# The program's first tile: loaded by two queues, normalised on three engines, with wk and the mix interleaved by block and wv split on GpSimd

## The reference

```
xn = layernorm(x)
xs = xn shifted by one token;  xm = xn*time_mix + xs*(1 - time_mix)
k = exp(min(xm @ Wk.T, 60));   v = xm @ Wv.T;   r = xm @ Wr.T
rwkv = sigmoid(r) * decayed_sum(k*v) / decayed_sum(k)
w_q = clip(round(W / mean|W|), -1, 1)
out = x + rwkv @ Wo.T + scaled(quantised(layernorm2(xn)) @ w_q)
```

## Time and profile before

| what | value |
|---|---|
| median of 3 runs (lowest to highest) | 893.41 us (892.99 to 894.22) |
| time of the profiled execution | 891.49 us |
| span of its instructions | 889.7 us |
| TensorE matmuls busy | 867.1 us, 97% |
| VectorE busy | 764.8 us, 86% |
| ScalarE, GpSimd busy | 510.3 us (57%), 215.2 us (24%) |
| DMA, mean over the span | 120 GB/s |

### The profile page before, as it was taken

The page is one execution under the profiler, slowest core; times in us unless marked ns, Lnnn a source line. Parts: engine busy times, 40 slices in busy tenths (PEclk is TensorE's granted clock), DMA queues, the critical chain, the costliest instruction groups (busy, mean ns, idle before and its releaser), DMA issues.

```text
span 889.7 us, 12792 instructions
## 1 busy us (share of the span) xinstructions
PE 867.1 (97%) x3984; PEld 714.5 (80%) x3984; DVE 764.8 (86%) x1278; ACT 510.3 (57%) x834; POOL 215.2 (24%) x242
## 2 busy tenths in 40 slices
PE   3989999999999999999999999999999999999998
PEld 2778888888888888888888888888888888888886
DVE  5998999989897999989897897878978888789684
ACT  5584767667594757566564554545546536365441
POOL 5552326242452425240030100200201103011000
PEclk9999999999999999999999999999999999999999
DMA  8222415041423224045643245324451443424311
GB/s 283 108 83 88 149 54 184 13 171 54 165 71 135 101 82 154 12 172 136 212 145 115 84 154 189 125 75 141 153 175 57 157 141 96 154 93 142 95 48 47
DMA packets 59841, 107.13 MB, mean 120 GB/s; under 512 B 7712, under 2 KB 7712, under 8 KB 59808
## 3 DMA queue, kind: packets, MB, share of 16 engines
q1 hardware_dynamic: 59808, 106.73, 35.1%
HBM read 64.76 MB, written 41.96 MB: 120 GB/s over the span
## 4 chain that ended last, share of the span: by engine, by line
PE 90%; DVE 3%; issue 2%; POOL 2%; ACT 1%; DMA 0%; SPq 0%; POOLq 0%; DVEq 0%; ACTq 0%
PE kvr L513 18%; PE kvr L515 18%; PE kvr L514 18%; PE out_banks L552 7%; PE out_banks L554 7%; PE out_banks L534 6%; PE out_banks L533 6%; PE out_banks L531 6%; PE transposed L466 2%; PE out_banks L466 2%; DVE bn_stats L842 1%; POOL normed L1174 1%; POOL own_stats L1156 1%; POOL own_stats L1157 1%; DMA x<-in_x 0%
## 5 line engine op out<-in xcount | busy, mean ns | idle before, releaser
L1247 POOL TENSOR_TENSOR evacuated<-normed,mix_over_ffn_row 128x512 f32<-128x512 f32 x28 | 49.0, 1751 | 339.0 <-DVE ffn_lo L922 339.0
L513 PE MATMUL kvr<-xm_hi,wk_hi 128*128 128x512 f32 x256 | 103.7, 405 | 2.6 <-DVE xm_lo L922 2.6
L513 PE MATMUL kvr<-xm_hi,wv_hi 128*128 128x512 f32 x256 | 102.9, 402 | 2.2 <-DVE wv_lo L927 1.3
L513 PE MATMUL kvr<-xm_hi,wr_hi 128*128 128x512 f32 x256 | 102.7, 401 | 0.0
L515 PE MATMUL kvr<-xm_hi,wk_lo 128*128 128x512 f32 x256 | 101.0, 395 | 0.0
L514 PE MATMUL kvr<-xm_lo,wk_hi 128*128 128x512 f32 x256 | 100.7, 394 | 0.0
L515 PE MATMUL kvr<-xm_hi,wv_lo 128*128 128x512 f32 x256 | 100.2, 391 | 0.0
L515 PE MATMUL kvr<-xm_hi,wr_lo 128*128 128x512 f32 x256 | 100.1, 391 | 0.0
L531 PE MATMUL out_banks<-wo_hi,rwkv_hi 128*128 128x512 f32 x256 | 100.0, 390 | 0.0
L534 PE MATMUL out_banks<-wo_hi,rwkv_lo 128*128 128x512 f32 x256 | 99.7, 389 | 0.0
L514 PE MATMUL kvr<-xm_lo,wr_hi 128*128 128x512 f32 x256 | 99.7, 389 | 0.0
(11 more groups left out here) (140 smaller groups left out, 1922.7 us busy)
## 6 DMA issues: line engine op xcount, KB each, us to landing
other<-ffn_input SPq DMA_DIRECT2D x64, 256.0 KB, 5.1
x<-in_x SPq DMA_DIRECT2D x15, 1024.0 KB, 5.8
other<-in_x SPq DMA_DIRECT2D x8, 1024.0 KB, 5.8
ffn_input<-evacuated SPq DMA_DIRECT2D x32, 256.0 KB, 4.4
ffn_input<-parked SPq DMA_DIRECT2D x32, 256.0 KB, 2.2
attn_scratch<-x SPq DMA_DIRECT2D x8, 1024.0 KB, 4.2
parked<-attn_scratch SPq DMA_DIRECT2D x8, 1024.0 KB, 6.7
out<-parked SPq DMA_DIRECT2D x8, 1024.0 KB, 5.2
```

The source lines that it names most:

```text
L513: nc.tensor.matmul(KVR[:, m, :], hi, XH[t][:, ch, :], start=(ch == 0), stop=False)
L1247: G.tensor_tensor(U[:, n % RING, :], XN[:, ch, :], BC[:, :], ALU.mult).then_inc(pool_v, 1)
```

## The change

The change touches the startup only, apart from waits that TensorE carries in every batch.

- **Loads.** SyncE issues blocks 0 and 2 of the first tile and then the constants; ScalarE issues blocks 1 and 3.
- **First normalisation.** VectorE takes blocks 0 and 1, GpSimd block 2, ScalarE block 3. The second normalisation (for the feed-forward input) of blocks 0 and 1 goes from GpSimd to VectorE.
- **Mix.** The shifted part is written into an own buffer `FIRST` of 513 columns whose first column is zero, so that one instruction per block takes the place of three. The P slots are transposed into the `out_banks`.
- **wk and mix.** ScalarE and VectorE split block m of wk between the steps of the mix; TensorE waits for wk's low part block by block.
- **wv.** The low part of wv moves from VectorE to GpSimd, behind its high part; a semaphore `pool_w` counts it. GpSimd splits wo only when `dve_w` shows wk and wr done. The reload of the second x tile waits for `pool_w`.

```diff
@@ nc.sync
+            for q in (0, 2):
+                sp.dma_start(X[0][:, q, :], x_t[0, 0][:, q, :]).then_inc(s_xq[q], 16)
             sp.dma_start(cst[:, :], constants).then_inc(s_small, 16)
-            for q in range(Q):
-                sp.dma_start(X[0][:, q, :], x_t[0, 0][:, q, :]).then_inc(s_xq[q], 16)
             for n in "kvr":
                 load_weight(n)
             sp.dma_start(ZA[:, :, :], x_t[HALF, 0]).then_inc(s_oth, 16)
             sp.wait_ge(dve_w, CH)
             load_weight("o")
-            sp.wait_ge(dve_w, 2 * CH)
+            sp.wait_ge(pool_w, CH)
             sp.dma_start(X[1][:, :, :], x_t[0, 1]).then_inc(s_x[1], 16)
@@ nc.tensor
-            for normed in (pool_xn, act_xn):
+            for normed in (dve_xn, pool_xn, act_xn):
                 pe.wait_ge(normed, CREDIT)
             for m in range(CH):
                 transpose_slot(0, "P", m, XN)
-            pe.wait_ge(dve_w, CH)
-            pe.wait_ge(dve_x, 2)
...
-                if m:
-                    pe.wait_ge(dve_w, (m + 1) * CH)
+                if m == 1:
+                    pe.wait_ge(pool_w, CH)
+                if m == 2:
+                    pe.wait_ge(dve_w, 2 * CH)
...
                         pe.wait_ge(dve_lo, RING + slots_before(b, ph, slot0 + ch) + 1)
+                        pe.wait_ge(dve_w, ch + 1)
@@ nc.scalar
+            for q in (1, 3):
+                nc.scalar.dma_start(X[0][:, q, :], x_t[0, 0][:, q, :]).then_inc(s_xq[q], 16)
...
-            weight_hi("k")
-            for m in range(CH):
+            weight_hi("k", [0])
+            evacuate(0, "P", 0)
+            weight_hi("k", [1])
+            evacuate(0, "P", 1)
+            high_part(0, "P", 0)
+            for m in range(2, CH):
+                weight_hi("k", [m])
                 evacuate(0, "P", m)
-            for m in range(CH):
-                high_part(0, "P", m)
+                high_part(0, "P", m - 1)
+            high_part(0, "P", CH - 1)
@@ nc.vector
-                    V.tensor_copy(last_x[:, ch:ch + 1], shifted(ph, n)[:, TILE - 1:TILE])
-                    V.tensor_scalar(U[:, r, 0:1], bank[:, 0:1], scale, None, ALU.mult)
-                    V.scalar_tensor_tensor(U[:, r, 1:TILE], bank[:, 1:TILE], scale, shifted(ph, n)[:, 0:TILE - 1],
+                    V.scalar_tensor_tensor(U[:, r, :], bank, scale, FIRST[:, n, 0:TILE],
                                            ALU.mult, ALU.add).then_inc(dve_x, 1)
...
-            weight_lo("k")
+            for q in range(2):
+                last = V.tensor_scalar(XN[:, q, :], X[0][:, q, :], own[:, 0, 0, q:q + 1], own[:, 0, 1, q:q + 1],
+                                       ALU.mult, ALU.add)
+            last.then_inc(dve_xn, 1)
+            weight_lo("k", [0])
             mix_or_clip(0, "P", 0)
             for m in range(1, CH):
+                weight_lo("k", [m])
                 mix_or_clip(0, "P", m)
                 low_part(0, "P", m - 1)
             low_part(0, "P", CH - 1)
-            weight_lo("v")
...
             weight_lo("r")
@@ nc.gpsimd
-            normalise(XN, X[0], own[:, 0], 0, pool_xn)
+            normalise(XN, X[0], own[:, 0], 0, pool_xn, [2])
             ffn_scale(0, 0, own[:, 0])
-            pool.wait_ge(pe_t, CH)
-            normalise(XN, X[0], own[:, 0], 1, pool_xn)
...
             for ch in range(CH):
                 G.tensor_copy(WH["v"][:, ch, :], RAW["v"][:, ch, :]).then_inc(hi_w["v"], 1)
+            for ch in range(CH):
+                pool.wait_ge(hi_w["v"], ch + 1)
+                G.tensor_tensor(WL["v"][:, ch, :], RAW["v"][:, ch, :], WH["v"][:, ch, :].bitcast(F32),
+                                ALU.subtract).then_inc(pool_w, 1)
+
+            pool.wait_ge(dve_w, 2 * CH)
             pool.wait_ge(s_w[3], 16)
```

More of the change, by code:

```diff
@@ L56 @@
 RING = 4
+FFN_ROOM = 176640
 BANK_USES = {"A": ["attn0", "attn1"],
@@ L203, in mixed_decay_kernel @@
         pool_v = sem("pool_mix_input")
+        pool_w = sem("pool_wv_lo")
+        dve_xn = sem("dve_first_normed")
         dve_past = sem("dve_past_wait")
@@ L287, in shifted @@
                 return (WS[:, 0, :], WS[:, 1, :], BC[:, :], WS[:, 0, :])[n % CH]
-            return E[:, n % 2, :] if ph == "P" and n > 1 else WS[:, n % 2, :]
-        first_banks = [TB[:, :]] + [KVR[:, i, :] for i in range(3)]
+            return FIRST[:, n, 1:TILE + 1] if ph == "P" else WS[:, n % 2, :]
+        first_banks = [OUT[:, q, :] for q in range(Q)]
         def slot_bank(ph, n):
@@ L492, in slot @@
                     else:
+                        pe.wait_ge(dve_xn, 2)
                         for normed in (pool_xn, act_xn):
@@ L520, in attn_out @@
                 first_bank = bank_use(b, ph, f"attn{t}")
-                pe.wait_ge(dve_w, 4 * CH)
+                pe.wait_ge(dve_w, 3 * CH)
                 for j in range(CH):
@@ L683, in _, with weight_hi @@
             NORMALISE_AT = {2: "ffn_other0", 6: "mix_own1", 14: "ffn_other1", 18: "mix_next0"}
-            def weight_hi(n):
+            def weight_hi(n, chunks=range(CH)):
                 act.wait_ge(s_w[names.index(n)], 16)
-                for ch in range(CH):
+                for ch in chunks:
                     nc.scalar.activation(WH[n][:, ch, :], RAW[n][:, ch, :], ACT.Copy).then_inc(hi_w[n], 1)
@@ L697, in _ @@
             act.wait_ge(pool_step, STEPS + MIX_STEPS)
[L698 to L701, removed]
+            nc.scalar.activation(XN[:, 3, :], X[0][:, 3, :], ACT.Identity,
+                                 bias=own[:, 0, 1, 3:4], scale=own[:, 0, 0, 3:4]).then_inc(act_xn, 1)
             act.wait_ge(dve_c, 2)
-            weight_hi("k")
-            for m in range(CH):
+            weight_hi("k", [0])
[5 more added lines that the diff above has]
+                weight_hi("k", [m])
                 evacuate(0, "P", m)
-            for m in range(CH):
-                high_part(0, "P", m)
+                high_part(0, "P", m - 1)
+            high_part(0, "P", CH - 1)
             act.wait_ge(pool_step, STEPS + STEPS)
@@ L713, in _ @@
             weight_hi("r")
-            act.wait_ge(dve_w, 3 * CH)
+            act.wait_ge(dve_w, 2 * CH)
             def exp_k(b, c):
@@ L832, in _ @@
             V.memset(mx[:, :], 0.0).then_inc(dve_mx, 1)
+            V.memset(FIRST[:, :, 0:1], 0.0)
             def stats_of(i, src, place, ph, first=False):
@@ L935, in _ @@
             low_part(0, "P", CH - 1)
-            weight_lo("v")
+            dve.wait_ge(pe_t, CH)
+            dve.wait_ge(pool_step, STEPS + STEPS)
+            dve.sem_inc(dve_past, 1)
+            for q in POOL_CHUNKS:
+                last = V.tensor_scalar(XN[:, q, :], X[0][:, q, :], own[:, 0, 2, q:q + 1], own[:, 0, 3, q:q + 1],
+                                       ALU.mult, ALU.add)
+            last.then_inc(dve_xn, 1)
             weight_lo("r")
+            V.tensor_copy(last_x[:, :], FIRST[:, :, TILE])
             def ternary_sum():
```

6 lines of the change are left out of this document (5 added, 1 removed).

## The result

| | before | after |
|---|---|---|
| median (lowest to highest) | 893.41 us (891.23 to 894.22, 9 runs) | 895.17 us (893.79 to 898.16, 9 runs) |
| span of the profiled execution | 889.7 us | 893.0 us |
| TensorE, VectorE, GpSimd busy | 867.1, 764.8, 215.2 us | 868.3, 766.2, 219.5 us |
| start of slot 8 | 52.31 us | 54.86 us |

A forecast was written before the change was run, and what follows sets the result against it. TensorE, busy 97% of the span, was taken as the bound, so only its startup waits could be won. 0.15 + 1.0 = 1.15 us gained took 893.4 to 892.3 us, range 890.2 to 895.6.

The forecast's parts named there:

- Step 2: First normalising and mix: transposes start at 12.7 us, the mix's last low part ends at 22.3 us against 21.99 before.
- for which I add 0.8: Allowance in us for GpSimd's casts stretching low parts in VectorE's 7.0 us chain of 11 operations.
- the interleaving works: Splitting wk between mix steps: slot 0 starts at about 23.6 instead of 24.12 us, the gain spent by late constants.
- Step 1: Loads and first statistics: constants come at 5.7 us, scale and bias at 11.3 instead of 10.2 us, 1.1 us lost.
- Step 3: wv's low part on GpSimd: four subtractions at 1.55 us each, v group starts at 25.9 to 26.0 instead of 26.11.
- strict turns: Rival, chance 0.17: GpSimd and VectorE alternate whole instructions during wv's subtractions, 7.6 us for four; 893.6 us, no change.
- 0.15 us gained: Forecast gain at the start of the v group from moving wv's low part to GpSimd.
- the rival of a starved GpSimd: Chance 0.18: VectorE leaves GpSimd no turn during wv's subtractions, 2.4 us each, wv ready at 29.3 us; 895.6 us.
- My argument against turns: In the kernel before, low parts and casts ran side by side at 1.10 and 0.96 us; strict turns would make 1.4.
- Step 4: VectorE's head start into the first batch: second tile's statistics earlier, slot 8 at 51.2 us, 1.0 us gained.
- the head start of 2.2 us: VectorE enters the first batch about 2.2 us earlier, with wo's low part at about 31.5 instead of 33.75 us.
- the matmuls' extra waits: The waits added to TensorE's matmuls in each batch were costed at nothing, each being met long before.

The follow-up runs named there:

- e3: The changed kernel with the four low-part subtractions of wv moved back from GpSimd to VectorE; ratio to the kernel before 1.0016.
- e5: The changed kernel with only the interleaving of wk and the mix undone; ratio to the kernel before 1.0026.
- e2: The changed kernel with VectorE's wait for the constants moved behind the first tile's statistics; ratio to the kernel before 1.0019.
- e4: The kernel before with only the changed loads (two queues, constants behind blocks 0 and 2); ratio to the kernel before 1.0017.
- e1: The changed kernel with the constants issued ahead of blocks 0 and 2 on SyncE; ratio to the kernel before 1.0021.
- e7: The changed kernel with the edits of e2, e3 and e5 together; ratio to the kernel before 0.9986.
- e9: e7 without GpSimd's wait for VectorE's slots ahead of the casts of wo; ratio to the kernel before 1.0013.
- e6: The changed kernel with the edits of e2 and e3 together, interleaving kept; ratio to the kernel before 0.9997.
- e10: e7 with the first normalising on two engines (GpSimd blocks 0 and 1, ScalarE 2 and 3); ratio to the kernel before 0.9995.
- e8: e4 with VectorE's wait for the constants moved behind the first tile's statistics; ratio to the kernel before 0.9989.

## Why the prediction was wrong

The forecast was 1.15 us faster; the kernel is some 3.2 us slower. At slot 8, where the sum was made, the forecast was 51.2 us and the trace has 54.86.

**Step 2 is the step that failed**: "7.0 us" of chain, "for which I add 0.8", last low part at 22.3 us. Counted from the first mix, at 15.24 us, the chain took 10.45 us and ended at 25.69: of the 3.4 us by which the last low part is late, 2.65 are the chain and 0.74 a later first mix (15.24 for 14.5). I had added the contention of GpSimd's casts to VectorE's chain, but that of the four subtractions only to GpSimd's own price. By e3 against after, that omission is 2.38 us: without the subtractions the chain took 8.07 us (15.51 to 23.58 in e3), near the 7.8 of the forecast. The second mistake is "the interleaving works": the old order had the four low parts of wk in time that VectorE spends waiting for TensorE and ScalarE anyhow (TensorE's transposes start at 12.13 us):

```profile
12.30 2.50 DVE L927 TENSOR_TENSOR wk_lo<-parked,wk_hi 128x512 fp32r<-128x512 f32 x4 [4.40 <-ACT wk_hi L689]
...
14.91 0.73 DVE L880 SCALAR_TENSOR_TENSOR evacuated<-transposed,constants,shifted_part 128x511 f32<-128x511 f32 x1
```

By e5 against after, that is 1.67 us; the two overlap, since each stretches the other (together 14.19 to 11.19, 3.0 us). The start of the transposes, 1.4 us after scale and bias, was 1.89: with the three engines starting together, GpSimd's operation takes 1.34 us.

**Step 1** was right in kind and close in size: constants used at 6.14 us, forecast 5.7, near the upper end of its interval (6.2; other profiles have up to 6.40); 1.30 us lost, forecast 1.1. e2 and e4 show it from both sides. The Trainium skill ("DMA: Bandwidth & Descriptors", Queues, rings and completion order) has the constants wait in their ring for the blocks ahead while another ring takes turns; the 4.5 us here against 1.8 agree with it, and so does e1, where the first block pays for ScalarE's two.

**Step 3**: the price of a subtraction was 1.69 us, forecast 1.55, with strict turns at 1.91; wv was ready at 26.83 instead of 25.9. It wasn't what the v group waited for in the end: the k group, late by VectorE's chain, ended after it. So neither "0.15 us gained" nor the rival of a starved GpSimd holds: that rival had the sign, but the engine that held up the v group was VectorE, and that the measured median, 895.2 us, lies next to its 895.6 is luck.

The two engines worked in turns. GpSimd's subtractions start at 20.08, 21.75, 23.43 and 25.11 us, and within each of them exactly one low part of VectorE ends, at 20.66, 22.34, 24.01 and 25.69 us. Only the pitch is shorter than the one that I called strict: 1.68 us, not 1.29 + 0.62 = 1.91. So a low part adds 0.39 us to a GpSimd subtraction, and a subtraction about 1.1 us to a low part. Whether those 0.2 us are sharing, or a part of each instruction's recorded time in which it needs nothing of the other's, the rows can't say. My argument against turns was wrong as well: I took 0.80 us for a cast, the mean of four of which two ran beside low parts (1.06 and 1.07 us; the others 0.60 and 0.61). Alone a cast takes 0.57 (four in 2.29, e7), so whole turns would be 1.2 us and not 1.4. In the kernel before, the low parts of wv start at 21.91, 22.93, 23.95 and 24.97 us and the casts of wo between them, at 22.42, 23.43 and 24.45: turns again, at a pitch of 1.02 us. The Trainium skill ("SBUF — State Buffer", SBUF: two separate sides) has the engine that starts first hold the shared port for the whole instruction while the other is blocked. The order of these rows agrees with it, and so does the mix that reads PSUM and keeps its 0.74 us.

**Step 4**: the head start of 2.2 us was a delay of 1.6 (wo's low part ends at 35.35 instead of 33.75 us). In all twelve profiles slot 8 starts either 22.3 us behind the r group, when TensorE is late (after, e1, e2, e9), or 18.6 to 18.7 us behind wo's low part, when VectorE is (the others). In the changed kernel TensorE was the later one, since its v group ran in part at 1.2 GHz: 0.94 us that no term of mine held (without them slot 8 would follow wo's low part, at about 54.0 us). That the matmuls' extra waits cost nothing was right: from 204 us on the distance to before is constant within 0.1 us.

**What stays open.** Two things behind slot 8 differ between runs of like kernels, and they are as large as what the experiments differ by in front of it. One is the wait of VectorE for a load of x: at 92 to 96 us it is 0.99 to 1.84 us in e2, e3, e4, e5, e6, e9 and e10 and absent in before, after, e1, e7 and e8; at 194 to 196 us it is 0.36 us in the changed kernel, 0.85 and 0.76 in e3 and e9, and absent before. So e4's profiled span is 3.3 us over before's, though its slot 8 is 1.50 late. The other is TensorE's clock: the windows of e7 and of e8 right behind slot 8, after waits of TensorE of 2.26 and 2.12 us:

```profile
50.00:54.00 4.00, 3.46 (x13) 2.88 (x14) 3.90 (x8) 3.19 (x6) 3.08 (x7) 0.72 0.89 311
54.00:58.00 4.00, 4.00 (x18) 3.24 (x18) 3.96 (x7) 2.43 (x4) 0.28 (x1) 0.86 0.00 0
```

```profile
50.00:54.00 4.00, 2.28 (x12) 2.00 (x13) 3.90 (x8) 3.69 (x7) 3.44 (x6) 1.00 0.76 278
54.00:58.00 4.00, 4.00 (x21) 3.28 (x20) 3.97 (x6) 3.32 (x6) 1.26 (x3) 1.00 0.22 56
```

In e7 the clock fell (0.72 and 0.86), in e8 it didn't. From slot 8 to the first sums of the attention output it is 28.0 us in e2, e3, e6, e7 and e9 and 26.5 to 26.7 in the others: 1.4 to 1.5 us. So e7's profiled span, 889.4 us, keeps little of its 1.77 us. Why the same wait ends in the lower clock in one profile and not in another, these runs don't show. Whether it is a property of the kernel is open, too: each has one trace here, and the mean granted clock differs between executions of one kernel. The ratios average over that; the table's times up to slot 8 stand in front of it.

## What to carry to other kernels

Compare startups at a fixed place behind them and not by the span of one trace. Price an elementwise operation that is moved to GpSimd twice: by what it takes there, and by what it adds to every SBUF-to-SBUF instruction that VectorE runs meanwhile, above all when VectorE's chain is the critical one; operations that read PSUM can stand beside it. Before interleaving two pieces of work, ask in which idle time the first one lies now, for interleaving takes it out. And a small load whose semaphore is waited for ahead of the bulk's work must be issued ahead of the bulk, or its wait moved behind.

## What the runs showed of the hardware

- VectorE's subtraction with two SBUF inputs, 128x512: 0.68 us alone, 0.99 to 1.10 beside a GpSimd cast, 1.09 to 1.77 beside a GpSimd subtraction (1.76 and 1.77 where it lay wholly beside one). Its normalisation: 0.54 alone, 1.48 to 1.50 beside a GpSimd subtraction (after, e5). GpSimd's subtraction 1.29 alone, 1.71 to 1.74 beside them, its normalisation 0.77 alone and 1.34 beside VectorE's.
- A load of 10 KB lands 1.8 us after its issue when first in its queue. Behind two blocks of x, with two more in another queue, it is used 4.3 to 4.8 us after its issue (after, e3, e4, e5).
- A wait of TensorE of 1.61 us (changed kernel) and one of 2.45 us (e9) went with a fall of its clock to 1.2 GHz, so a wait can cost more than it lasts: 0.94 us in the changed kernel's v group, 1.6 us in e9's. Waits of 1.55 us ahead of e7's v group and of 2.1 to 2.3 us ahead of slot 8 in seven profiles went with none.
- The trace's own record of the clock can begin late. The k group of the kernel before runs at 0.63 us a matmul from 18.9 to 24.1 us, the pace of the lower level, while its windows show 1.00; but the record of the clock in that trace begins only at 24.36 us, and the 1.00 ahead of it stands for no reading. In e5 it begins at 24.63 us, and the matmuls go from 0.63 us (23.18) over 0.48 (24.45) to 0.39 (24.76). Ahead of the first record the pace of the matmuls is what tells the clock, and by it the kernel before ran its k group at the lower level, too.
